# Attention in two halves: GpSimd's sum left out, TensorE multiplies both halves of a query product

## What is computed

```python
q = l2_normalize(xn @ qw.T)
k = l2_normalize(xn @ kw.T)
v = xn @ vw.T
# heads(): 16 heads of 8 values
diff = n - m
dmask = jnp.where(causal[None], gammas[:, None, None] ** exponent[None], 0.0)
sim = jnp.einsum('bhnd,bhmd->bhnm', qh, kh) * scale
sim = sim * dmask[None]
yh = jnp.einsum('bhnm,bhmd->bhnd', sim, vh)
y = y @ ow.T + ob
```

## Time and profile before

| what | us |
|---|---|
| median of 3 runs | 561.37 |
| lowest and highest | 559.96, 561.92 |
| the profiled execution | 563.65 |
| its span, from the first to the last instruction | 561.4 |
| busy in the span: TensorE, VectorE | 472.2, 428.1 |
| busy in the span: GpSimd, ScalarE | 346.9, 344.0 |

### The profile page before, as it was taken

How to read it: one execution, slowest core, us unless ns; L and a number is a source line. 1 busy time by engine, 2 the same in 40 slices (tenths; PEclk the granted TensorE clock), 3 DMA queues, 4 the chain that set the end, 5 groups by cost and what they waited for, 6 DMA issues and landing times. The chain is left out here.

```text
span 561.4 us, 6822 instructions
## 1 busy us (share of the span) xinstructions
PE 472.2 (84%) x2334; PEld 330.9 (59%) x2334; DVE 428.1 (76%) x705; ACT 344.0 (61%) x463; POOL 346.9 (62%) x249
## 2 busy tenths in 40 slices
PE   4989798799999999989798997978988948577766
PEld 4456566435778887667675585865676723133324
DVE  5769999973442424049898799998899998899995
ACT  1444352424573565589998999987999816744410
POOL 3127988937313044205678758798658799789662
PEclk9979988989899999999999999999999967869999
DMA  8800000000000000401775751856752856952100
GB/s 288 321 1 0 1 1 1 1 0 0 1 1 1 1 2 4 149 1 37 180 160 142 179 132 63 200 132 152 169 132 76 187 131 152 212 126 75 56 0 20
DMA packets 15602, 48.95 MB, mean 87 GB/s; under 512 B 2320, under 2 KB 7824, under 8 KB 12624
## 3 DMA queue, kind: packets, MB, share of 16 engines
q0 software_dynamic: 3024, 22.02, 19.4%
q1 hardware_dynamic: 11968, 25.58, 13.7%
q10 hardware_dynamic: 576, 0.92, 0.5%
HBM read 25.31 MB, written 1.18 MB: 47 GB/s over the span
## 5 line engine op out<-in xcount | busy, mean ns | idle before, releaser
L1396 PEld LDWEIGHTS pO<-w_e,gel 128*128 128x128 f32 x1024 | 122.0, 192 | 13.7 <-issue 8.8
L1396 PE MATMUL pO<-w_e,gel 128*128 128x128 f32 x1024 | 124.8, 276 | 0.9 <-DVE X L796 0.6
L825 DVE TENSOR_TENSOR_SCAN Hs<-dA,HL,pCT 128x512 f32<-128x512 f32 x96 | 117.7, 1267 | 7.1 <-POOL ZS L397 3.6
L1083 ACT ACTIVATE gel<-pH,b_e 128x512 f32<-128x512 f32 x128 | 86.3, 687 | 40.0 <-PE pH L1386 39.2
L397 POOL TENSOR_TENSOR ZS<-Hs,Crow 128x1024 f32<-128x1024 f32 x31 | 74.9, 2430 | 27.5 <-DVE Hs L825 26.0
L1095 ACT ACTIVATE dA<-dt,a_neg 128x512 f32<-128x512 f32 x128 | 81.9, 711 | 10.3 <-DVE Hs L825 10.0
L812 DVE TENSOR_TENSOR pCT<-u,pB 128x1024 f32<-128x1024 f32 x64 | 78.3, 1224 | 10.4 <-PE pB L1476 9.3
L1384 PE MATMUL pH<-h2h,w_e1h 128*128 128x512 f32 x128 | 58.2, 455 | 19.8 <-ACT gel L1083 18.7
L796 DVE SCALAR_TENSOR_TENSOR X<-pO,wts,X 128x128 f32<-128x128 f32 x128 | 36.0, 344 | 44.8 <-PE pO L1396 44.1
L397 POOL TENSOR_TENSOR Zev<-Hs,Crow 128x1024 f32<-128x1024 f32 x26 | 62.7, 2416 | 8.8 <-DVE Hs L825 8.5
L1476 PE MATMUL pB<-ST,sel 96*128 96x512 bf16 x64 | 26.1, 409 | 35.4 <-DVE pCT L812 35.3
(11 more groups left out here) (261 smaller groups left out, 859.0 us busy)
## 6 DMA issues: line engine op xcount, KB each, us to landing
Crow<-c_rows SPq DMA_DIRECT2D x32, 512.0 KB, 4.1
Acc<-ZS POOLq DMA_DIRECT2D x12, 1024.0 KB, 8.6
Acc<-Zev POOLq DMA_DIRECT2D x9, 1024.0 KB, 7.1
w_e<-in_w_e SPq DMA_DIRECT2D x2, 2048.0 KB, 10.9
X<-in_x SPq DMA_DIRECT2D x4, 256.0 KB, 6.9
S<-in_w_mod ACTq DMA_DIRECT2D x2, 384.0 KB, 5.1
out<-h2T SPq DMA_DIRECT2D x3, 256.0 KB, 2.8
w_cx<-in_conv_row SPq DMA_DIRECT2D x1, 512.0 KB, 9.7
```

The lines of the kernel that those rows point to most:

```text
L825: vec.tensor_tensor_scan(Hs[:, 2 * o + d, 0:w], dA[:, 4 * (p % 2) + 2 * o + d, 0:w], pU[:, d, 0:w], HL[:, d, n:n + 1] if c else 0.0, ALU.m ...
L1083: nc.scalar.activation(gel[:, n % NG, 0:w], pH[n % 2][:, 0:w], ACT.Gelu_apprx_tanh, bias=b_e1[:, NK * e + k:NK * e + k + 1]).then_inc(s["m ...
L1396: ins = mm(pO[:, j * P:(j + 1) * P], gel[:, n % NG, j * P:(j + 1) * P], w_e2[:, NK * (g % E) + k, :], start=(k == 0 and j == 0), stop=(k = ...
```

## The change

GpSimd's sum of the two halves goes, and `ZAs` with it. `ZA` has four slices in place of two, so that products take turns in its two halves. TensorE multiplies both halves of every pair by `w_o` and adds them up in PSUM, as it did for the last pair alone. The wait for output product R - 2 moves from the sum to the front of the product. VectorE's own product of pair 15 writes the second half of `ZA` and waits for output product 13 instead of for the last sum.

```diff
-        ZA = sbe("ZA", [P, 2, TC])
-        ZAs = sbe("ZAs", [P, 2, TC])
+        ZA = sbe("ZA", [P, 4, TC])
...
                     pool.wait_ge(s["att_qs"], R + 1)
                     pool.wait_ge(s["att_sc"], 2 * R + 2)
-                    if R:
-                        pool.wait_ge(s["att_zs"], R)
-                    pool.tensor_tensor(ZA[:, :, :], Qsb[:, 2 * (R % 2):2 * (R % 2) + 2, :], S[:, 2 * r:2 * r + 2, :],
-                                       ALU.mult).then_inc(s["att_zo"], 1)
-                    pool.wait_ge(s["att_zo"], R + 1)
                     if R >= 2:
                         pool.wait_ge(s["att_ow"], R - 1)
-                    pool.tensor_tensor(ZAs[:, R % 2, :], ZA[:, 0, :], ZA[:, 1, :], ALU.add).then_inc(s["att_zs"], 1)
+                    pool.tensor_tensor(ZA[:, 2 * (R % 2):2 * (R % 2) + 2, :], Qsb[:, 2 * (R % 2):2 * (R % 2) + 2, :],
+                                       S[:, 2 * r:2 * r + 2, :], ALU.mult).then_inc(s["att_zo"], 1)
...
             vec.wait_ge(s["att_qs"], NR * NC)
-            vec.wait_ge(s["att_zs"], NR * NC - 1)
-            vec.tensor_tensor(ZA[:, :, :], Qsb[:, 2:4, :], S[:, DH - 2:DH, :], ALU.mult).then_inc(s["att_zl"], 1)
+            vec.wait_ge(s["att_ow"], NR * NC - 2)
+            vec.tensor_tensor(ZA[:, 2:4, :], Qsb[:, 2:4, :], S[:, DH - 2:DH, :], ALU.mult).then_inc(s["att_zl"], 1)
...
                 if R == NR * NC - 1:
                     pe.wait_ge(s["att_zl"], 1)
-                    mm(pO[:, :], w_o[:, :], ZA[:, 0, :], start=False, stop=False)
-                    mm(pO[:, :], w_o[:, :], ZA[:, 1, :], start=False, stop=True).then_inc(s["att_ow"], 1)
-                    return
-                pe.wait_ge(s["att_zs"], R + 1)
-                mm(pO[:, :], w_o[:, :], ZAs[:, R % 2, :], start=(r == 0), stop=(r == NR - 1)).then_inc(s["att_ow"], 1)
+                else:
+                    pe.wait_ge(s["att_zo"], R + 1)
+                for i in range(2):
+                    ins = mm(pO[:, :], w_o[:, :], ZA[:, 2 * (R % 2) + i, :], start=(r == 0 and i == 0), stop=(r == NR - 1 and i == 1))
+                ins.then_inc(s["att_ow"], 1)
```

## The result

| what | before | changed |
|---|---|---|
| median of 5 runs, us | 560.26 | 566.74 |
| lowest to highest, us | 559.96 to 561.92 | 566.32 to 569.89 |
| profiled execution, us (span) | 563.65 (561.4) | 569.89 (567.7) |
| busy: TensorE, VectorE, GpSimd, us | 472.2, 428.1, 346.9 | 479.3, 426.9, 328.0 |

The ratio is 1.0092, with a 95% interval of 1.0062 to 1.0122: slower by 5.2 us by the ratio (3.5 to 6.8). A second set of runs gave 1.0094 (1.0063 to 1.0126). Single executions scatter: those of the kernel before lie between 558.94 and 564.92 us in all sets.

A forecast was written before the change was run, and what follows sets the result against it. VectorE was taken to bound attention, its last output-product reading setting when later work starts. At full clock 1.5 + 0.8 + 1.0 - 1.5 = +1.8 us; with half-clock stretches +3.2, median 564.6 us, range 561.4 to 567.4.

The forecast's parts named there:

- the forecast's own case: Attention: one or two of three half-clock stretches of TensorE stay; 564.6 us (563.6 to 565.8), chance 0.55.
- the three places: Attention, near 68, 92 and 112 us: TensorE at half clock after idle waits; some stretches should go, which was open.
- finish: After a chunk's fourth pair, three times: VectorE reads the doubled output product 0.5 us late; +1.5 us.
- norms' operation: VectorE's tiny operation at 68.50 and 90.98 us no longer waits for GpSimd to let go; -1.5 us.
- rests of keys and queries: Next chunk's first pair, twice: rounding rests reach VectorE 0.4 us late behind TensorE's added work; +0.8 us, bounds 0 and 1.2.
- the end: Last pairs of attention: GpSimd's product 14 waits for output product 12, so the last output product ends later; +1.0 us.
- half clock: spread and key row behind it: Attention: remaining half-clock stretches delay VectorE; +1.3 near 68 us, +0.8 or +1.6 near 92, +1.7 near 112.
- a case by a rule of the Trainium skill: End of attention: VectorE's last product stands still until GpSimd's product 14 is over, ending at 117.3 us; sum unchanged.
- The later finish: TensorE's waits before half clock: added work shortens them to about 0.7 us, but 0.5 comes back in two.
- The clock stays full: Rival, attention: added passes fill TensorE's pauses and all three half-clock stretches go; +1.0 us, 562.4, chance 0.21.
- all stretches stay: Rival, attention: all three half-clock stretches stay, or VectorE's delays open longer pauses; +5.6 us, 567.0, chance 0.18.
- GpSimd was the pace-maker: Rival, attention: 19.1 us less of GpSimd shorten the stage; -1.3 us at most, 560.1 or below, chance 0.06.

The follow-up runs named there:

- r8: The kernel before, unedited, for a second trace: attention part 85.92 us, 442.59 us behind it.
- r9: The changed kernel, unedited, for a third trace: attention part 90.24 us, 442.73 us behind it.
- r2: The changed kernel with three buffers of GpSimd's products in place of two, so each waits for an output product one pair further back: ratio 1.0075 to the kernel before.
- r3: The kernel before, GpSimd's sums and waits kept, with TensorE multiplying each sum by the output matrix twice: ratio 1.0069 to the kernel before.
- r10: The kernel before, unedited, for a third trace: attention part 85.74 us, 441.42 us behind it.
- r1: The changed kernel run again without an edit: ratio 1.0094 to the kernel before, attention part 90.44 us.
- r4: The changed kernel with only the first half of each product multiplied by the output matrix, except for the last pair: ratio 1.0007 to the kernel before.
- r5: The changed kernel with the output product ahead of the second key row in each chunk's second and third pair: ratio 0.9979 to the kernel before.

## Why the prediction was right

It said 564.6 us, slower by 3.2, from waits on TensorE in attention. The way and the mechanism came as said, and the time lies inside the range, but the loss is larger than forecast: 5.2 us by the ratio, and in attention 3.4 us between the first two traces, 4.15 between the means of three. The median of 566.74 us lies outside the forecast's own case (563.6 to 565.8) and next to the rival's 567.0 by which all stretches at half clock stay. The traces speak against that rival: one or two of the three places are at half clock in each of them. What makes up the difference are several smaller terms and some 1 us behind attention. Against r8 (85.92), r9 (90.24) can be taken apart without the stretch at the start, which both lack. VectorE in r8:

```profile
49.77 0.69 DVE L680 TENSOR_TENSOR vp<-pB,rb 128x512 f32<-128x512 f32 x1 [0.29 <-ACT rb L987]
50.90 0.70 DVE L709 TENSOR_TENSOR pH<-pH,vp 128x512 f32<-128x512 f32 x1 [0.44 <-PE pH L1244]
...
66.64 0.64 DVE L673 SCALAR_TENSOR_TENSOR nrm<-nrm 128x8 f32<-128x8 f32 x1
...
88.05 0.75 DVE L673 SCALAR_TENSOR_TENSOR nrm<-nrm 128x8 f32<-128x8 f32 x1
...
93.46 0.69 DVE L680 TENSOR_TENSOR vp<-pB,rb 128x512 f32<-128x512 f32 x1 [0.47 <-ACT rb L987]
94.90 0.70 DVE L709 TENSOR_TENSOR pH<-pH,vp 128x512 f32<-128x512 f32 x1 [0.75 <-PE pH L1244]
...
113.55 1.23 DVE L727 TENSOR_TENSOR ZA<-Qsb,S 128x1024 f32<-128x1024 f32 x1
116.91 0.70 DVE L686 SCALAR_TENSOR_TENSOR pO<-pO,rb 128x512 f32<-128x512 f32 x1 [2.14 <-PE pO L1254]
```

And in r9, besides the waits at the finishes (0.67, 0.67, 0.55) and the norms' operation (0.17 twice):

```profile
54.31 0.70 DVE L704 TENSOR_TENSOR pH<-pH,vp 128x512 f32<-128x512 f32 x1 [0.26 <-PE pH L1239]
...
57.24 0.69 DVE L660 TENSOR_TENSOR qk_lo<-pY,qk_hi 128x512 fp32r<-128x512 f32 x1 [0.18 <-ACT q L972]
...
72.47 0.69 DVE L675 TENSOR_TENSOR vp<-pB,rb 128x512 f32<-128x512 f32 x1 [1.24 <-ACT rb L982]
...
77.68 0.70 DVE L704 TENSOR_TENSOR pH<-pH,vp 128x512 f32<-128x512 f32 x1 [0.38 <-PE pH L1239]
...
80.61 0.69 DVE L660 TENSOR_TENSOR qk_lo<-pY,qk_hi 128x512 fp32r<-128x512 f32 x1 [0.18 <-ACT q L972]
...
96.02 0.69 DVE L675 TENSOR_TENSOR vp<-pB,rb 128x512 f32<-128x512 f32 x1 [1.42 <-ACT rb L982]
...
101.23 0.70 DVE L704 TENSOR_TENSOR pH<-pH,vp 128x512 f32<-128x512 f32 x1 [0.38 <-PE pH L1239]
...
116.51 1.75 DVE L722 TENSOR_TENSOR ZA<-Qsb,S 128x1024 f32<-128x1024 f32 x1 [0.26 <-PE pO L1251]
120.97 0.70 DVE L681 SCALAR_TENSOR_TENSOR pO<-pO,rb 128x512 f32<-128x512 f32 x1 [2.71 <-PE pO L1251]
```

| term | forecast | r9 against r8 |
|---|---|---|
| finish | +1.5 | 0.67 + 0.67 + 0.55 = +1.89 |
| rests of keys and queries, with the key row ahead at full clock | +0.8 | 0.26 + 2 x 0.18 = +0.62 |
| the end | +1.0 | (0.26 + 2.71 + 1.75) - (2.14 + 1.23) = +1.35 |
| norms' operation | -1.5 | 2 x 0.17 - 0.64 - 0.75 = -1.05 |
| half clock: spread and key row behind it | +1.4 | (1.24 + 0.38 + 1.42 + 0.38) - (0.29 + 0.44 + 0.47 + 0.75) = +1.47 |
| sum | +3.2 | +4.28 of 4.32 |

Finish, end and norms' operation came out 0.35 to 0.45 us worse each, 1.2 us together, the rests 0.2 better.

**Finish.** Right in place, 0.4 us short.

**Rests.** Nearly right in sum, but VectorE pays a part of it earlier than forecast, on the key row in front of the subtractions (0.26 us at 54.31, at full clock, with no half clock ahead of it in that trace); at the rests themselves 0.18 us are left.

**The end.** Right in its cause, 0.35 us short: with a third buffer 1.1 us go (r2). VectorE's own last product takes 1.75 us in place of 1.23: it starts at 118.67 in the first trace, while GpSimd's product 14 runs from 116.99 to 119.34, and ends 1.08 us behind it (the case had 1.2). I had this as a case by a rule of the Trainium skill (SBUF — State Buffer, "Who interferes with whom"), with the statement that the sum would stay; TensorE's output products 14 and 15 run through without a gap from 119.40 on, so it did.

**Norms' operation.** The mechanism is shown, by its length with and without a GpSimd instruction beside it (r3: 0.86 and 0.17; every changed trace: 0.17). It needn't be the sum: at 66.64 in r8 it ends at 67.28, together with GpSimd's product (64.92 to 67.27). The size was read from the longest trace; in r8 and r10 it is 0.64 to 0.75, so the gain is 1.0 us.

**Clock.** The sum is near the forecast (1.5 against 1.4 us), but in part by luck, since three steps of it don't hold.
- The later finish was said to give 0.5 us back to two of the three waits. It precedes the third as well, so all three are 1.2 us long, where 0.7 was worked out for one.
- That shorter waits take stretches away isn't shown. Of the three places the kernel before has three, two and two at half clock in its three traces, the changed kernel one, two and one. In r8 a wait of 1.56 us (at 109.47) is followed by full clock, in the changed kernel one of 1.24 us by either.
- A stretch in front of a spread costs the changed kernel 1.6 to 1.9 us each time (1.24 to 1.56 on the spread, 0.38 on the key row behind it), also near 92 us when VectorE is already late, where 0.8 was forecast. Such a stretch stands near 46 us too in r1, which the forecast had not. On the other side the kernel before pays more than the 0.81 us of the trace that the price was set against: 1.95 us in r8 and 1.79 in r10.

The prediction's list of VectorE's waits in the stage also leaves out the 2.47 and 0.98 us at 39.53 and 41.21. They come from a stretch at half clock from 33.3 us on, ahead of all output products, in some executions of either kernel.

**The rivals.** "The clock stays full" didn't come in any of three traces, and neither did "all stretches stay", though the median is where it said. "GpSimd was the pace-maker" is refuted by r4. Some 1 to 2 us of the measured loss are not in attention: the forecast took the rest of the kernel as unchanged, and named a change of it as a sign of being wrong. Up to some 436 us it kept its length, the part behind did not in some traces, and whether that belongs to the change stays open.

## What to carry to other kernels

Work taken from an engine with slack was worth nothing that could be measured here (r4), and the same work given to one that the bounding engine reads from was paid where the reading stands right behind it: look for the place in the order, not at the sum of idle time. Some 13 us more of TensorE (15 times 1.88 less 1.02) cost 5 us in one order and nothing measurable in another, with the output product moved in front of the instruction at which TensorE waited anyway. When a wait is moved from a short instruction to the long one in front of it, look where the next stage drains, since only there no later work hides it; and take more than one trace of the kernel before, since one had 2 us more in this stage than the others, and the traces of one kernel differ in where its clock falls.

## What the runs showed of the hardware

- TensorE's granted clock was 0.50 in one or more stretches of 3.4 to 6.8 us of the attention part in every trace but that of r5, at different places in executions of the same kernel: the kernel before has its first at 33.3 us in one trace and at 46.2 and 45.4 in the others. The attention parts of these three are 87.85, 85.92 and 85.74 us, while the medians of its three larger sets lie between 560.26 and 561.89.
- VectorE's operation on the norms, two inputs of 8 values for each partition in SBUF, takes 0.17 us, and 0.64 to 1.05 us where it meets a sum or product of GpSimd; it ends together with that instruction (69.55 and 69.53 in the first trace, 68.62 and 68.59 in r3, 67.28 and 67.27 in r8). VectorE's product of 1024 elements takes 1.23 us alone and 1.75 where GpSimd's product runs for its first 0.67 us; it ends 1.08 us behind that one.
